# Slot rows in chunk 5, five gate rows on ScalarE, the first weights split at every second chunk, and the gate columns in chunk 5 of the first unit

## What is computed

```
s0 = relu(x @ swi[0]) @ swo[0]                    # 256 -> 1024 -> 256, in fp32
s1 = relu(x @ swi[1]) @ swo[1]
eo = relu(x @ wi[label]) @ wo[label]              # one expert per sample
w  = softmax(relu(concat(eo[:, 0], s0[:, 0], s1[:, 0]) @ g1) @ g2)
x  = x + eo * w[:, 0] + s0 * w[:, 1] + s1 * w[:, 2]
out = x + zX * lap_x(x) + zY * lap_y(x) + zR * x * (1 - x)
```

## Time and profile before

| | us |
|---|---|
| median of 3 runs | 1157.97 |
| lowest, highest | 1157.39, 1158.76 |
| the profiled execution | 1157.13 |
| its span, from first to last instruction | 1155.6 |
| PE busy in the span | 1136.1 |
| DVE, ACT busy | 675.7, 454.1 |

### The profile page before, as it was taken

How to read it: one execution, slowest core, us unless ns; L and a number is a source line. 1 busy time by engine, 2 the same in 40 slices (tenths; PEclk the granted TensorE clock), 3 DMA queues, 4 the chain that set the end, 5 groups by cost and what they waited for, 6 DMA issues and landing times.

```text
span 1155.6 us, 16650 instructions
## 1 busy us (share of the span) xinstructions
PE 1136.1 (98%) x5988; PEld 967.3 (84%) x5988; DVE 675.7 (58%) x1019; ACT 454.1 (39%) x798; POOL 72.7 (6%) x111
## 2 busy tenths in 40 slices
PE   8999999999999999999999999999999999999995
PEld 7788888888888888888888888888888888888884
DVE  6756665656666644546556555555565565465564
ACT  2655555545555532333333323323423333333232
POOL 1111111111111100000000000000000000000001
PEclk9999999999999999999999999999999999999998
DMA  7555456556555514023023022121131231230200
GB/s 241 170 161 166 145 158 194 154 146 180 159 171 153 158 37 112 18 66 83 16 68 81 12 74 47 45 74 31 57 79 24 60 83 21 63 83 15 69 28 28
DMA packets 109986, 107.78 MB, mean 93 GB/s; under 512 B 78320, under 2 KB 86736, under 8 KB 109904
## 3 DMA queue, kind: packets, MB, share of 16 engines
q1 hardware_dynamic: 96832, 60.04, 19.3%
q0 software_dynamic: 12800, 46.41, 13.5%
q10 hardware_dynamic: 272, 0.26, 0.1%
HBM read 85.20 MB, written 17.04 MB: 88 GB/s over the span
## 4 chain that ended last, share of the span: by engine, by line
PE 97%; DVE 1%; issue 1%; DMA 0%; SPq 0%; ACT 0%; DVEq 0%; POOL 0%; POOLq 0%; ACTq 0%
PE acc L808 31%; PE hbank L784 16%; PE hbank L783 16%; PE acc L809 16%; PE hbank L785 16%; PE tbank L740 1%; PE acc L707 0%; DMA y<-y 0%; PE acc L797 0%; PE tbank L735 0%; PE tbank L748 0%; PE tbank L741 0%; DVE hf L538 0%; SPq L1090 0%; DVE swo L574 0%
## 5 line engine op out<-in xcount | busy, mean ns | idle before, releaser
L541 DVE SCALAR_TENSOR_TENSOR hl<-hbank,hh 128x512 fp32r<-128x512 f32 (+2 forms) x432 | 274.2, 635 | 438.5 <-ACT hh L884 438.1
L884 ACT ACTIVATE hh<-hbank 128x512 fp32r<-128x512 f32 (+2 forms) x432 | 238.8, 553 | 599.1 <-PE hbank L785 596.2
L808 PE MATMUL acc<-swo,hh 128*128 128x512 f32 x1024 | 370.9, 396 | 0.0
L809 PE MATMUL acc<-swo,hl 128*128 128x256 f32 x1024 | 286.8, 280 | 0.0
L808 PEld LDWEIGHTS acc<-swo,hh 128*128 128x128 f32 x1024 | 192.3, 188 | 45.4 <-DVE eo L559 0.2
L783 PE MATMUL hbank<-xh,swh 128*128 128x512 f32 x512 | 202.6, 396 | 0.0
L784 PE MATMUL hbank<-xl,swh 128*128 128x512 f32 x512 | 202.3, 395 | 0.0
L809 PEld LDWEIGHTS acc<-swo,hl 128*128 128x128 f32 x1024 | 193.1, 189 | 9.9
L785 PE MATMUL hbank<-xh,swl 128*128 128x512 f32 x512 | 199.2, 389 | 0.0
L808 PE MATMUL acc<-ewo,hh 128*128 128x512 f32 x528 | 194.5, 398 | 0.3
L809 PE MATMUL acc<-ewo,hl 128*128 128x256 f32 x528 | 148.0, 280 | 0.0
(11 more groups left out here) (176 smaller groups left out, 846.1 us busy)
## 6 DMA issues: line engine op xcount, KB each, us to landing
rw<-in_L_cond_wi POOLq DMA_DIRECT2D x44, 512.0 KB, 4.4
rw<-in_L_cond_wo POOLq DMA_DIRECT2D x44, 512.0 KB, 4.6
xs<-in_x SPq DMA_DIRECT2D x128, 64.0 KB, 3.2
eo_scratch<-eo SPq DMA_DIRECT2D x128, 64.0 KB, 2.5
xs<-in_x SPq DMA_DIRECT2D x16, 512.0 KB, 4.4
rw<-in_x SPq DMA_DIRECT2D x256, 32.0 KB, 2.2
ei<-eo_scratch SPq DMA_DIRECT2D x16, 512.0 KB, 5.5
out<-ot SPq DMA_DIRECT2D x15, 512.0 KB, 6.3
```

The source lines that it names most:

```text
L541: e.scalar_tensor_tensor(HL[:, g % NH, 0:w], bank[:, 0:w], 0.0, HH[:, g % NH, 0:w].bitcast(F32), ALU.max, ALU.subtract).then_inc(h_lo, 1)
L808: e.matmul(acc[j][:, 0:2 * D], HH[:, g % NH, js], woc[:, c, :], start=(c == 0), stop=False)
L809: m = e.matmul(acc[j][:, D:2 * D], HL[:, g % NH, js], woc[:, c, 0:D], start=False, stop=last)
L884: e.activation(HH[:, g % NH, 0:w], hbank[g % HRING][:, 0:w], ACT.Relu).then_inc(h_hi, 1)
```

## The change

`ROWS_AT` goes from 4 to 5: the slot rows on PE and the slot table on DVE stand one chunk later. `EARLY` goes from 4 to 5: ACT also brings out the hidden values of chunk 4, and since `HF` has four slots, it now waits there for slot 0 to be free. The splittings of shared network 0 are spread from chunks 4, 5, 6, 7 to 5, 7, 9, 11, and the first part of the first unit's weights goes from chunk 15 to 14. The gate columns move from chunk 2 of the first unit to chunk 5, on PE and on DVE.

```diff
-ROWS_AT = 4
+ROWS_AT = 5
-EARLY = 4
+EARLY = 5
...
-    if (_n, _c) == (2, 2):
+    if (_n, _c) == (2, 5):
         T_ORDER.append("gate s")
...
-FIRST_CUTS = {(0, 4): [(0, 0)], (0, 5): [(0, 2)], (0, 6): [(0, 1)], (0, 7): [(0, 3)], (1, 7): [(2, 0)], (2, 0): [(2, 2)],
+FIRST_CUTS = {(0, 5): [(0, 0)], (0, 7): [(0, 2)], (1, 1): [(0, 1)], (1, 3): [(0, 3)], (1, 6): [(2, 0)], (2, 0): [(2, 2)],
               (2, 1): [(1, 0), (2, 1)], (2, 2): [(1, 1)], (2, 3): [(2, 3)], (2, 4): [(1, 3)], (2, 7): [(1, 2)]}
...
                 if g < EARLY:
                     e.wait_ge(h_prod, g + 1)
-                    e.activation(HF[:, g, :], hbank[g % HRING][:, 0:128], ACT.Relu).then_inc(h_early, 1)
+                    if g >= NH:
+                        e.wait_ge(*h_free(g - NH))
+                    e.activation(HF[:, g % NH, :], hbank[g % HRING][:, 0:128], ACT.Relu).then_inc(h_early, 1)
```

More of the change, by code:

```diff
@@ L650, in _ @@
                         tile_low_whole(next_tile(n, c - 1))
-                if (n, c) == (2, 2):
+                if (n, c) == (2, 5):
                     e.wait_ge(t_prod, T_AT["gate s"])
```

## The result

| us | before | changed |
|---|---|---|
| median | 1158.05 (22 runs) | 1156.16 (22 runs) |
| lowest, highest | 1156.43, 1158.78 | 1155.18, 1160.17 |
| the profiled execution | 1157.13 | 1156.41 |
| its span | 1155.6 | 1154.9 |

The ratio of the times is 0.9986, with a 95% interval of 0.998 to 0.9993: a gain of 1.6 us (0.8 to 2.3), at the edge of what can be told from no change and inside the forecast range. The two profiled executions differ by 0.72 us, where the sum said 0.67. The medians differ by more, 1.9 us.

A forecast was written before the change was run, and what follows sets the result against it. PE was taken as the bound, busy 1136.1 of 1155.6 us, with gains only in the first 36 us. -1.06 + 0.39 = -0.67 us took the median from 1157.97 to 1157.3, range 1155.5 to 1159.0.

The forecast's parts named there:

- the sum: Over the whole kernel: -1.06 us at the second unit's transposes plus 0.39 for the gate transposes, giving -0.67 us.
- 1. Rows a chunk later: First small pass: slot rows start at 12.27 instead of 11.72, DVE's table ends 0.55 us later, PE gains 0.33 us.
- 2. DVE's rounds: Small passes from 14.3: waits before second products 6 and 7 vanish, product 8 starts at 18.2, 1.85 us won.
- 3. ACT's splittings behind its loads: Second small pass: two splittings wait for ACT's load issue until 18.2, PE waits for `hf` 10, 0.8 us given back.
- 4, 5. First unit and product 16: First weights in time, unit starts at 26.5 instead of 27.59; without gate columns product 16 at 32.45 instead of 34.37.
- 6. x(2) as the new limit: Second unit's transposes, wanted at 33.85, wait for SP's last x(2) load: 34.7 instead of 35.76, 1.06 us remain.
- (a): Rival at the second unit: x(2) lands by 33.85, total -1.5 us (chance 0.15), or -2.3 without ACT's delay (0.10).
- 7. The gate columns: Chunk 5 of the first unit: the four transposes now lie in a stretch without holes and cost PE 0.39 us.
- the last term: From profiled execution to median: the 0.84 us by which the profiled execution before lay below its median, kept after the change.
- (b): Rival at the second unit: x(2) takes 5.9 us to land, transposes at 35.6, total +0.2 us; chance 0.12.
- (c): Rival between 25.5 and 34.7: PE falls to its slow pace after idling, costing 4.9 us, total +4.2; chance 0.07.
- (d): Rival in the small passes: DVE's relief wins nothing, first unit's transposes stay at 24.94 or later, total -0.46 us; chance 0.06.

## Why the prediction was right, point by point

**1. Rows a chunk later.** Predicted at 12.27, measured 11.49, after an idle of 0.97 for `msel`: the start was the quick one. L455 is at 12.92, done at 13.13 (predicted 13.90, before 13.35). In executions with the slow start the rows stand about where the step put them: 12.09 with the earlier x(2), 12.43 with ACT's splittings ahead as well. With the earlier x(2) the table was done at 13.72, so later than before by 0.37 and not 0.55.

**2. DVE's rounds.** Right: no idle before second products 6 and 7. Product 8 is at 17.48, and 18.2 was predicted for a slow start.

**3. ACT's splittings behind its loads.** Right, with an idle of 5.18 until the loads are out, two L915 behind it, and a wait of PE of 0.57 (predicted 0.8). The kernel with the splittings ahead has no such wait.

**4, 5. First unit and product 16.** Right. The kernel with the earlier x(2) gives 26.45 and 32.44 for 26.5 and 32.45, and the idle before product 16 is 1.55 (predicted 1.6).

**6. x(2) as the new limit.** The idle of 1.08 before L740 that only a DMA ends is there, and without the wait in SP's queue it is gone. The time, 34.58 for 34.7, was luck: two errors cancel. The step made the queue later because the slot table is later. In this execution the table and the issue of x(1)'s last load (17.04, before 17.27) were 0.2 us earlier, but that load took 5.7 us to land instead of 4.4, and so x(1) was there at 22.8 (predicted 22.2) and x(2)'s last load went out at 30.12 (predicted 29.6). That one took 4.3 us instead of 5.0. Which transfer is last is right, but the delay of such a load is known only to a us or two: x(2)'s last load took from 2.8 to 7.0 us in these kernels. "DMA: Bandwidth & Descriptors" of the Trainium skill, on the anatomy of one DMA by GpSimd's path, would have made 2.15 of it (an estimate from its fixed cost and bandwidth). The last load comes down to that in no profile; the first of the eight in the earlier trace rows did (2.1). The text of this step also names the wrong rival: the one meant is (a), the first.

**7. The gate columns.** 0.35 to the next product (predicted 0.39), and 0.47 in all for the distance between the two L740.

**The sum** for the profiled execution is -0.67, measured -0.72. Its terms were -1.06 and +0.39, measured -1.18 and +0.47. That they meet so closely is luck too: 0.23 of the 0.72 is the quick start, which the sum doesn't hold, and from t0 the gain is 0.48. What was mis-sized is the last term. The prediction took the distance of the profiled execution to the median, 0.84, as the same for both kernels. It is 0.92 before and -0.25 after. The distance holds the executions with the fallen clock: of the kernel before 41 of 90 have a mean clock of 0.994 or less, of the changed kernel 2 of 22 (those took 1158.87 and 1160.17). The median of 1157.3 was predicted from a term that the change itself altered; it is 1156.16. Among executions without a low clock the medians are about 1157.15 and 1156.0, so that some 1.2 of the 1.9 us are there and 0.7 goes with the low clocks. The 1.2 is still more than the 0.67 of the sum. A different share of quick starts would do that, but the start is known only for profiled executions, and this stays open. Nor does the clock explain every long execution: ACT's splittings ahead has one of 1158.36 and x(2) behind the small loads one of 1158.53, both at 0.996.

**The rivals.** (a) falls for the changed kernel, and it is what happens where SP doesn't wait. (b) didn't occur. (c) is real, but on the other side: it was in the kernel before, by the mean clocks in about half of its executions, with a price of 1.57 us rather than 4.9. The earlier trace rows are from an execution without it, and from them it could not be seen. The three times given for the kernel before, 1.4 us apart, were a hint. (d) falls: the transposes of the first unit came at 23.21 and not at 24.94, and product 16 came 2.5 us earlier.

**Which part takes the falls away** is not settled. Counted by a mean clock of 0.994 or less, they are frequent with the slot rows in chunk 4: before 41 of 90, gate columns alone 4 of 11, splittings alone 5 of 11. With the rows in chunk 5 they are rare: 6 of 103 executions over nine kernels. The wait of 1.87 for `s` in front of L827, behind which the fall in the one profile stands, is kept in the kernel with the gate columns put back (1.87) and in the one with the later rows alone (1.88), and these have 1 of 11 and 2 of 11. So that wait alone isn't the cause. What the later rows do change in a quick start is the wait for `msel`, 1.83 with the rows in chunk 4 (the kernel with the splittings alone) and 0.97 after. Whether this is why the clock holds was not tested. That the gate columns alone shift the median by 1.15 us, with none of eleven executions above 1157.1 although four have a low mean clock, is open too.

## What to carry to other kernels

When a stretch is tightened, work out for every transfer into it when its last piece was issued and how long that row took to land: here a queue that had been hidden by 1.7 us became the last to come, and undoing its needless wait brought the median down by another 0.85 us. A DMA issue in a compute engine's program is work of that engine: what is put behind it waits. If the executions of a kernel differ by more than the effect that is sought, look at more than one of them: the profiled one was neither the typical nor the only kind, and 0.7 of the 1.9 us gained in the median went with another kind. Compare profiles from a common event, here PE's first product: a start that was 0.23 us earlier had made a gain of 0.48 look like one of 0.72.

## What the runs showed of the hardware

- The same program has executions with and without a fall of TensorE's granted clock: 0.56 and 0.59 in 4 us behind an idle of 1.87 us, in two other executions 1.00 behind the same idle. The cost was 1.57 us.
- At the start PE ran at half pace up to about 10.1 us in half of the profiles (first products 0.43 us apart, later 0.22), while the granted clock of the page reads full.
- Loads whose address is read from a table are issued 0.975 us apart on SP (of which 0.27 is a row for reading the number and 0.49 the issue), and ACT's four took 3.56 us.
- A load of 64 KB took 2.1 us to land as the first of x(2)'s eight and 2.8 to 7.0 us as the last, beside GpSimd's loads of weights, and one that was issued 0.7 us later landed 0.9 us earlier.
